# Octonion FFN with an FFT attention on Trainium2: dot products, normalising and the request of x moved within a down unit's turn

## The reference

```python
x = L0_attn_x
xn = _layernorm(x, axis=-1)
x = x + _L0_attn_ref(xn) + _L0_ffn_ref(xn, w_gate, w_up, w_down)
```

## Time and profile before

| | |
|---|---|
| median of 3 runs | 609.52 us (609.05 to 611.1) |
| the profiled execution | 609.28 us, its span 607.5 us |
| granted TensorE clock, mean | 0.994 |
| instructions in the trace | 16365 |
| ScalarE, VectorE, GpSimd busy | 355.4, 507.7, 463.0 us |
| VectorE waiting for `normalise` (L937 on L604) | 12.0 us in 6 places |
| TensorE waiting for VectorE's second adds (L375 on L1026) | 4.3 us in 6 places |

### The profile page before, as it was taken

How to read it: one execution, slowest core, us unless ns; L and a number is a source line. 1 busy time by engine, 2 the same in 40 slices (tenths; PEclk the granted TensorE clock), 3 DMA queues, 4 the chain that set the end, 5 groups by cost and what they waited for, 6 DMA issues and landing times.

```text
span 607.5 us, 16365 instructions
## 1 busy us (share of the span) xinstructions
PE 580.5 (96%) x6728; PEld 539.8 (89%) x6728; DVE 507.7 (84%) x1229; ACT 355.4 (59%) x497; POOL 463.0 (76%) x362
## 2 busy tenths in 40 slices
PE   4898999979999999999999999999999999999996
PEld 4898998869989998899989998899989998998896
DVE  3885897969899989989888989989898989967854
ACT  4777867664557646765466545774476545543540
POOL 2404839998769977999769977999779977987920
PEclk9999999998999999999999999999999999999999
DMA  6720012001040012102040013002040112002021
GB/s 163 200 71 1 1 29 113 3 1 70 3 139 1 3 71 87 54 1 71 2 140 2 25 48 136 4 3 71 2 140 1 38 36 71 2 2 71 1 71 72
DMA packets 10235, 30.67 MB, mean 50 GB/s; under 512 B 912, under 2 KB 4016, under 8 KB 10160
## 3 DMA queue, kind: packets, MB, share of 16 engines
q1 hardware_dynamic: 9200, 28.22, 13.8%
q10 hardware_dynamic: 960, 1.40, 1.1%
HBM read 21.23 MB, written 8.39 MB: 49 GB/s over the span
## 4 chain that ended last, share of the span: by engine, by line
POOL 53%; issue 30%; PE 12%; DMA 2%; DVE 1%; ACT 0%; ACTq 0%; POOLq 0%
POOL hop L1320 15%; POOL hs L1314 10%; POOL hs L1315 10%; POOL hs L1310 9%; POOL hs L1309 6%; PE acc L470 5%; PE acc L395 4%; DMA hop<-in_w_gate 2%; PE acc L375 1%; PE acc L447 1%; POOL r L1268 1%; POOL hop L1317 1%; PE acc L404 0%; PE acc L368 0%; ACTq L570 0%
## 5 line engine op out<-in xcount | busy, mean ns | idle before, releaser
L470 PE MATMUL acc<-wd,hop 114*128 114x128 f16 (+1 forms) x2944 | 171.4, 220 | 1.0 <-POOL hop L1320 0.7
L470 PEld LDWEIGHTS acc<-wd,hop 114*128 114x128 f16 (+1 forms) x2944 | 168.3, 98 | 2.2 <-POOL hop L1320 0.9
L679 ACT ACTIVATE pk<-acc 114x512 f32<-114x512 f32 (+1 forms) x120 | 70.8, 590 | 71.7 <-PE acc L470 34.0
L1309 POOL TENSOR_TENSOR hs<-hx 114x512 f32<-114x512 f32 x47 | 60.2, 1282 | 68.3 <-DVE hx L1075 60.3
L1320 POOL TENSOR_TENSOR hop<-hs,hop 114x1024 f16<-114x1024 f32 x46 | 98.2, 2135 | 7.9 <-ACT hop L734 7.9
L1317 POOL TENSOR_TENSOR hop<-hx,hop 114x1024 f16<-114x1024 f32 x46 | 98.3, 2137 | 0.7 <-ACT hop L723 0.7
L375 PE MATMUL acc<-xop,wg 128*128 128x256 f16 x704 | 84.1, 273 | 4.5 <-DVE acc L1026 4.3
L723 ACT ACTIVATE hop<-hx 114x1024 f16<-114x1024 f32 x46 | 48.6, 1057 | 65.4 <-DVE hx L1075 65.4
L368 PE MATMUL acc<-xop,wg 128*128 128x256 f16 x704 | 84.2, 273 | 1.0 <-DVE hx L1075 0.9
L375 PE MATMUL acc<-xop,wu 128*128 128x256 f16 x704 | 84.1, 273 | 0.7
L368 PE MATMUL acc<-xop,wu 128*128 128x256 f16 x704 | 84.1, 273 | 0.7 <-DVE hx L1075 0.7
(11 more groups left out here) (163 smaller groups left out, 922.2 us busy)
## 6 DMA issues: line engine op xcount, KB each, us to landing
xr<-in_x SPq DMA_DIRECT2D x16, 512.0 KB, 5.0
zx<-in_x SPq DMA_DIRECT2D x16, 512.0 KB, 3.9
out_y<-zx SPq DMA_DIRECT2D x16, 512.0 KB, 2.9
hop<-in_w_down SPq DMA_DIRECT2D x1, 1364.0 KB, 6.3
hop<-in_w_gate ACTq DMA_DIRECT2D x1, 1152.0 KB
hop<-in_w_up SPq DMA_DIRECT2D x1, 1152.0 KB
hop<-in_w_gate ACTq DMA_DIRECT2D x1, 192.0 KB
hop<-in_w_up SPq DMA_DIRECT2D x1, 192.0 KB
```

Source lines behind the costliest of these rows:

```text
L470: last = nc.tensor.matmul(acc[:, bank[n], s // 2, at:at + P], operand(g, c, t, form, level), wd[0:WIDE[c], slot, c, :], start=which == 0 a ...
L679: nc.scalar.activation(pk[0:rows, q % 2, :, :], pair[:, :, T:2 * T], ACT.Copy, scale=XS if u[0] == "X" else 1.0).then_inc(copied, 1)
L1309: nc.gpsimd.tensor_tensor(hs[:, 4:8:2, :], h[:, 0:4:2, :], h[:, 1:4:2, :], ALU.add)
```

## The change

Three moves, no instruction added or taken away:

- SyncE: at the second tile of group g, for g = 1 to 4, x of group g + 3 is requested ahead of the wait for that tile's output and not behind the output's store. For g = 0 the order stays.
- ScalarE: the two `normalise` of a unit N stand behind `odd_two` (the copy of its odd sums), and no longer at the beginning of its turn.
- VectorE: the two `dot` of a unit N stand at the end of its turn, behind the second adds, and no longer ahead of its first adds.

```diff
@@ SyncE
             for g in range(G):
                 for t in range(NT):
                     k = NT * g + t
+                    if t == 1 and 0 < g and g + 3 < G:
+                        load_x(g + 3)
                     sp.wait_ge(out_done, k + 1)
                     sp.dma_start(out_rows[k, :, :], zx[:, t, :]).then_inc(out_st, 16)
-                    if t == 1 and g + 3 < G:
-                        load_x(g + 3)
+                    if t == 1 and g == 0:
+                        load_x(3)
                     if g < G - 1:
@@ ScalarE
             for n in range(OPEN, N + 8):
-                if n in norm_at:
-                    normalise(norm_at[n], 0)
-                    normalise(norm_at[n], 1)
                 if n in z_at:
...
                     if u[0] in "GUNX":
                         odd_two(u)
+                    if n in norm_at:
+                        normalise(norm_at[n], 0)
+                        normalise(norm_at[n], 1)
                     if u[0] == "X":
                         x_high(u)
@@ VectorE
                 if kind == "X":
                     x_low(u)
-                if n in norm_at and kind == "N":
-                    dot(norm_at[n], 0)
-                    dot(norm_at[n], 1)
                 if u in quad_no:
                     first_adds(n, u)
...
                 if u in sums_no:
                     second_adds(n, u)
+                if n in norm_at:
+
+                    dot(norm_at[n], 0)
+                    dot(norm_at[n], 1)
                 if kind == "R":
```

## The result

| | before | changed |
|---|---|---|
| median of 6 runs | 609.29 us (608.56 to 612.55) | 615.18 us (614.15 to 615.85) |
| span of the profiled execution | 607.5 us | 612.3 us |
| granted TensorE clock, mean | 0.994 | 0.998 |

The ratio is 1.0097, with a 95% interval of 1.007 to 1.0124: the change makes the kernel 5.9 us slower (4.3 to 7.6).

A forecast was written before the change was run, and what follows sets the result against it. TensorE, working 96% of the span, was taken as the bound. 8.5 us more in five steady groups less 2.3 in the first made 6.2 on top of 609.28 or 609.52: 615.6 us, range 608.6 to 620.

The forecast's parts named there:

- The place that decides: Steady groups: a later first add of U(g,1,0) delays TensorE equally, as pauses of 0.9 us before U(g,1,1) and G(g,2,0).
- The move of the normalising, 0.45: ScalarE at N(g-1,0): normalising between the two copies makes the add of U(g,1,0) 0.45 us later at the earliest.
- The dots, up to 1.7: End of N(g-1,0)'s turn: the second dot waits for GpSimd; U(g,1,0)'s add comes 1.7 us later, 8.5 in five groups.
- The stretch, 0.88 or whole: Second dot beside GpSimd: waits for its whole instruction (taken), or rival, stretched by only 0.88 us: 611.4 us, chance 0.10.
- The first group, -2.3: First group (g = 1): the 3.04 us pause goes, later dots cost some back, G(1,2,0) comes 2.3 us earlier.
- from there 9.2 to the product's start: First group: from the second dot's end at 135.4, VectorE's run takes 9.2 us to the product ahead of G(1,2,0).
- x requested earlier, 0: SyncE's loads of x, issued earlier, could help only the row sums, which show 0.1 us idle; costed at nothing.
- The sum: Whole kernel: 8.5 - 2.3 = 6.2 us slower, forecast 615.6 us, chance 0.52 for its own range 613.5 to 617.5.
- The second dot did not slip in: Rival at N(g-1,0): the second dot gets ahead of GpSimd's instruction or is not held up; 608.9 to 609.5 us, chance 0.15.
- TensorE's clock did not fall: Rival: the granted clock falls after the new pauses in six groups, up to 10 us on top, 617 to 626; chance 0.16.
- The third rival: Front of N: U(g,1,0)'s add comes earlier, five pauses of 0.17 and the first group's 3.04 go; 603.9 us, chance 0.07.

The follow-up runs named there:

- The run with the rounding moved: The changed kernel with ScalarE's rounding L736 one turn later in the first group alone, behind the copy for G(1,1,1): 614.61 us, ratio 1.0106.
- x requested earlier: The kernel before with only SyncE's request of x moved as in the change: 608.76 us, ratio 1.0007.
- normalising alone: The kernel before with only the normalising moved behind the copy, the dots staying in front: 634.42 us, ratio 1.0417.
- the runs with the normalising in front: The changed kernel with dots ahead of N(g-1,1)'s first adds, normalising back in front in all groups or all but the first: 606.91 and 606.06 us.
- the split kernel: The changed kernel with GpSimd's L1323 cut into two instructions of half the length, for all hidden units: 610.91 us, ratio 1.0047.

## Why the prediction was right, step by step

- **The place that decides.** Right: all added time in the steady groups stands before U(g,1,1) and G(g,2,0), nothing after the spectrum. Forecast 0.9 and 0.9, found 0.92 and 0.87.
- **The move of the normalising, 0.45.** Right in kind, too high: 0.29 per group is left where the dots are elsewhere. The forecast took VectorE's run up to the product as free of idle time, but there was slack of some 0.12 us in it, too short to show as a wait. Kernel before:

```profile
279.61 0.60 ACT L679 ACTIVATE pk<-acc 114x512 f32<-114x512 f32 x1
...
280.24 0.42 DVE L978 TENSOR_TENSOR bd<-acc,pk 114x256 f32<-114x256 f32 x1
```

VectorE's last output instruction began at 279.86, and this add of G(g,1,1) 0.38 later; in the changed kernel, where VectorE is the late one, the next add follows that instruction after 0.25. The other 0.04 of the difference is not explained.
- **The dots, up to 1.7.** The second dot came as forecast: 0.79 behind the first (forecast 0.81), 0.26 behind L1323 (0.3), 2.43 long (2.4). The add of U came 1.66 later after the copy of N (7.64 us, before 5.98). The same slack of 0.12 took the effect on the product to 1.53. The term was 8.5 and measured 7.6.
- **The stretch, 0.88 or whole.** The choice for the whole of GpSimd's instruction was the right one; cutting that instruction in two showed it. That is also what the Trainium skill's page SBUF — State Buffer says under "Who interferes with whom", and the trace agrees: 0.68 to 0.69 us for a free dot, 1.46 behind an instruction of 1.18, 2.43 behind one of 2.14.
- **The first group, -2.3.** By the two traces the gain was 1.57. This term failed in two ways. Its step "from there 9.2 to the product's start" took the run of VectorE's work to be free of waits as in a steady group. In the first group GpSimd starts late, the rounding L736 idles 5.08 for it, and the copy for G(1,1,1) stands behind that: 0.88 us of idle time. The run with the rounding moved shows it. And the value it was compared with is not firm. Three kernels with the same pause of 3.04 there (before, x requested earlier, normalising alone) took 23.60, 22.90 and 22.00 us; in the first two the granted clock fell (a mean of 0.93 over 24 us), in the third it stayed at 1.00. So the change, with its 22.03, gains 0.9 to 1.6 us there where the clock would have fallen and nothing where not.
- **x requested earlier, 0.** Right.
- **The sum.** 6.2 us were forecast, 5.9 measured. That it came this near is in part luck: both terms were too large, with opposite signs (7.6 less 0 to 1.6 is 6.0 to 7.6), and the medians hang on how often the clock fell in each kernel. Where it fell in neither, the change costs some 7 to 8 us (614.2 and 614.3 against 606.2 to 607.1).
- **The rivals.** The second dot did not slip in, though the margin was the 0.3 us that was named. TensorE's clock did not fall after pauses of 0.9 in the profiled execution (1.00 over each of these stretches), and the other five, with means of 0.995 to 0.998, have no room for a fall in every group. The third rival reckoned with five pauses of 0.17 to be won; the runs with the normalising in front show that they could not be.

## What to carry to other kernels

Before an instruction with two operands in SBUF is moved on VectorE, look at what GpSimd will be doing at the new place: the price is not its own duration but the rest of the GpSimd instruction that has begun, and where two such instructions follow each other with a semaphore between, GpSimd can get in again. The place for it is one where the engine idles anyway for something that arrives later; here that was one unit N further on. And a wait that looks like the end of one chain may be the end of two of nearly equal length: look at what arrives second before counting on it as a gain.

## What had not been expected

- The same pause of 3.04 us was followed by a fall of the granted clock in two of three profiled executions, and two pauses of 1.88 and 1.84 by none. Pauses of 1.41 and 2.39 were followed by one, and the wait of 4.53 in the opening went with one. A single profiled execution does not tell what a pause costs; how the mean clock spreads over all executions tells more.
- GpSimd's instruction of half the size took 1.18 and 1.16 us where the whole took 2.14: cutting it costs some 0.2 us, which the split kernel paid 46 times. In its steady groups no new pause shows for it; before N(0,0)'s last chunk the wait for GpSimd is 1.19 and not 0.91.
- Of the three moves, two alone were worse by 13 and 25 us and together by 6; the parts of a change do not add.
